# A two-layer graph network kernel: each node number in the count matrix is split at 128 instead of 98

## The reference

```
layer 0:  x_t = mlp(x);  e_t = mlp(edge_attr)
          aggregated = segment_sum(x_t[src] * e_t, dst)
          x = layernorm(x + layernorm(x + aggregated) * gamma + beta)
layer 1:  loops added; deg = segment_sum(1, dst)
          h = x;  twice: h = segment_sum(w[edge] * h[dst], src), w from deg of src and dst
          x = layernorm(x + h @ W.T + b)
```

## Time and profile before

| what | value |
|---|---|
| time, median of 3 runs | 7911.91 us (7910.12 to 7913.29) |
| the profiled execution's own time | 7922.12 us |
| its span in the profile | 7920.4 us |
| PE busy | 6220.9 us (79%) |
| PE weight loads busy | 5013.7 us (63%) |
| DVE busy | 4907.6 us (62%) |
| ACT busy | 4014.2 us (51%) |
| POOL busy | 3681.7 us (46%) |
| SP's DMA queue, share of 16 engines | 91.5% |
| packets under 512 B | 2152641 of 2451761 |

### The profile page before, as it was taken

One profiled execution on the slowest core, in us unless ns is written; L12 is line 12 of the kernel. 1 busy time (PEld: TensorE's weight loads), 2 busy tenths in 40 slices (PEclk: granted clock), 3 DMA queues, 4 the chain that ended last, 5 costly groups with the idle time before them and its releaser, 6 DMA issues.

```text
span 7920.4 us, 153799 instructions
## 1 busy us (share of the span) xinstructions
PE 6220.9 (79%) x51112; PEld 5013.7 (63%) x51113; DVE 4907.6 (62%) x6884; ACT 4014.2 (51%) x6632; POOL 3681.7 (46%) x3315
## 2 busy tenths in 40 slices
PE   6567776777776777777777777777389999999999
PEld 3455555555554555555555555555279999999998
DVE  3566666666666666667776767676745555455554
ACT  1444444444444444444444444444257767666665
POOL 0776666666666666666676666666010000100000
PEclk9665666666666666666666666666599999999999
DMA  3899999999999999999999999999566666666665
GB/s 114 56 72 69 72 70 71 72 68 71 69 71 71 68 71 71 68 72 68 71 68 68 68 69 67 69 67 70 37 183 199 196 188 198 199 185 186 188 190 160
DMA packets 2451761, 809.65 MB, mean 102 GB/s; under 512 B 2152641, under 2 KB 2378105, under 8 KB 2451049
## 3 DMA queue, kind: packets, MB, share of 16 engines
q1 hardware_dynamic: 2317110, 677.47, 91.5%
q0 software_dynamic: 107552, 121.32, 17.1%
q10 hardware_dynamic: 27018, 9.90, 0.5%
HBM read 590.00 MB, written 218.34 MB: 102 GB/s over the span
## 4 chain that ended last, share of the span: by engine, by line
PE 42%; SPq 40%; DVE 6%; ACT 4%; issue 3%; DMA 3%; POOL 1%; ACTq 0%; DVEq 0%; POOLq 0%
SPq L495 40%; PE bank L935 13%; PE compared L935 7%; PE sums L426 4%; PE compared L870 4%; PE bank L857 3%; PE sums L935 3%; PE bank L838 3%; DVE U L1198 2%; ACT arena L671 2%; DMA arena<-counts 1%; POOL arena L574 1%; PE bank L851 1%; ACT U L653 1%; ACT arena L739 1%
## 5 line engine op out<-in xcount | busy, mean ns | idle before, releaser
L574 POOL DMA_INDIRECT arena<-node_rows,arena x3125 | 3480.4, 1114 | 1895.1 <-issue 916.7
L671 ACT ACTIVATE arena<-compared 128x392 uint8<-128x392 f32 x3936 | 1749.6, 498 | 1719.9 <-PE compared L870 1327.9
L870 PE MATMUL compared<-U 128*128 128x98 bf16 x15744 | 1572.0, 256 | 1229.9 <-ACT arena L671 878.2
L870 PEld LDWEIGHTS compared<-U 128*128 128x128 bf16 x15744 | 1087.1, 120 | 1733.5 <-ACT arena L671 1193.8
L739 ACT ACTIVATE arena<-arena 128x1792 bf16<-128x1792 uint8 x868 | 1470.1, 1696 | 706.4 <-DMA arena<-counts 370.0
L1287 DVE CAST arena<-arena 128x1792 bf16<-128x1792 uint8 x868 | 947.5, 1094 | 998.1 <-PE sums L935 629.2
L935 PE MATMUL bank<-arena 128*128 x13888 | 1448.9, 248 | 0.0
L1198 DVE TENSOR_TENSOR U<-iota_share,arena 128x2048 bf16<-128x2048 bf16 x984 | 1197.4, 1217 | 93.1 <-PE compared L870 93.1
L935 PEld LDWEIGHTS bank<-arena 128*128 128x128 bf16 x13888 | 1187.6, 99 | 2.4
L935 PE MATMUL compared<-arena 128*128 x6944 | 1151.4, 248 | 42.6 <-DMA arena<-hop_parts,first_dst 25.0
L1198 DVE TENSOR_TENSOR U<-iota_b,arena 128x1568 bf16<-128x1568 bf16 x984 | 950.0, 965 | 0.0
(11 more groups left out here) (193 smaller groups left out, 3925.8 us busy)
## 6 DMA issues: line engine op xcount, KB each, us to landing
arena<-counts SPq DMA_DIRECT2D x1736, 224.0 KB
counts<-arena SPq DMA_DIRECT2D x124, 1568.0 KB, 6.5
arena<-in_edge_attr SPq DMA_DIRECT2D x125, 448.0 KB
arena<-node_rows,arena POOLq DMA_INDIRECT x3125, 17.4
hop_parts<-arena ACTq DMA_DIRECT2D x14, 672.0 KB, 5.2
arena<-in_x_t SPq DMA_DIRECT2D x13, 256.0 KB, 2.7
node_rows<-H SPq DMA_DIRECT2D x1, 3136.0 KB, 16.5
edge_rows<-arena SPq DMA_DIRECT2D x1, 3125.0 KB
```

What stands on the lines that cost most here:

```text
L574: e.indirect_dma_start(out=rows[:, q, k, :], out_offset=None, in_=node_rows, in_offset=bass.IndirectOffsetOnAxis(ap=src_i[:, t:t + 1], axi ...
L671: nc.scalar.activation(stage[:, k, v:v + VB, :].rearrange("p v n -> p (v n)"), compared[:, c % 2, 0:VB * B], ACT.Copy).then_inc(s_ev, 1)
L870: mm = nc.tensor.matmul(compared[:, c % 2, n * B:(n + 1) * B], HOH[:, j % 2, VB * c + n, :], BOH[:, j % 2, VB * c + n, :], start=True, sto ...
```

## The change

Before, high = n div 98 (0 to 127) and low = n mod 98 (0 to 97). Now high = n div 128 (0 to 97) and low = n mod 128. The stationary matrix of a row's product, the one-hot of the high digit, has 98 columns instead of 128, and the moving one has 128 instead of 98. The product has 98 partitions of 128 numbers instead of 128 partitions of 98. A fill is 98 x 512 instead of 128 x 392, and a block's store consists of 98 x 128 pieces of 128 bytes instead of 128 x 128 pieces of 98 bytes. The digits are now made with a shift and a mask. `stage` grows into the space of `raw`, which is not in use then, and the zero tile for the last, empty block is half as long and lies elsewhere.

```diff
-        STAGE_W = 2 * P * B // 4
-        stage = place_in_arena(STAGE_W).bitcast(u8).rearrange("p (q v n) -> p q v n", q=2, n=B)
+        STAGE_W = 2 * P * P // 4
+        stage = place_in_arena(STAGE_W).bitcast(u8).rearrange("p (q v n) -> p q v n", q=2, n=P)
...
-        ZW = COLS // 4
-        zero_t = arena[:, AT_RAW:AT_RAW + ZW // 4].bitcast(u8)
+        ZW = COLS // 8
+        zero_t = arena[:, AT_EA + EA_W:AT_EA + EA_W + ZW // 4].bitcast(u8)
...
-        HOH = U_flat[:, 0:V * P].bitcast(bf16).rearrange("p (q v e) -> p q v e", q=2, e=P)
-        BOH = U_flat[:, V * P:V * P + V * B].bitcast(bf16).rearrange("p (q v e) -> p q v e", q=2, e=B)
+        HOH = U_flat[:, 0:V * B].bitcast(bf16).rearrange("p (q v e) -> p q v e", q=2, e=B)
+        LOH = U_flat[:, V * P:2 * V * P].bitcast(bf16).rearrange("p (q v e) -> p q v e", q=2, e=P)
...
             def store_block(k, q):
                 e.wait_ge(s_ev, last_use(k) + (1 + 2))
-                e.dma_start(counts[bass.ds(k * P, P), :].rearrange("v (a b) -> a v b", b=B), stage[:, q, :, :])\
+                e.dma_start(counts[bass.ds(k * P, P), :].rearrange("v (a b) -> a v b", b=P), stage[0:B, q, :, :])\
                     .then_inc(s_cst[q], 16)
...
-                    nc.scalar.activation(stage[:, k, v:v + VB, :].rearrange("p v n -> p (v n)"),
-                                         compared[:, c % 2, 0:VB * B], ACT.Copy).then_inc(s_ev, 1)
+                    nc.scalar.activation(stage[0:B, k, v:v + VB, :].rearrange("p v n -> p (v n)"),
+                                         compared[0:B, c % 2, :], ACT.Copy).then_inc(s_ev, 1)
...
-                        mm = nc.tensor.matmul(compared[:, c % 2, n * B:(n + 1) * B], HOH[:, j % 2, VB * c + n, :],
-                                              BOH[:, j % 2, VB * c + n, :], start=True, stop=True)
+                        mm = nc.tensor.matmul(compared[0:B, c % 2, n * P:(n + 1) * P], HOH[:, j % 2, VB * c + n, :],
+                                              LOH[:, j % 2, VB * c + n, :], start=True, stop=True)
...
-            link(nc.vector.tensor_scalar(whole, src_g[0:G, :], 1.0 / B, -(B - 1) / (2.0 * B), ALU.mult, ALU.add))
...
+            for n, (op, by) in enumerate(((ALU.arith_shift_right, 7), (ALU.bitwise_and, P - 1))):
+                link(nc.vector.tensor_scalar(digit[n][0:G, :], src_g[0:G, :], by, None, op))
+                node_leaky(2 + 2 * n, 3 + 2 * n)
+                link(nc.vector.tensor_scalar(table_part(P + n * (P // 2)).bitcast(bf16), by_tile(digit[n][0:G, :]),
+                                             (1.0 / P, 1.0)[n], None, ALU.mult))
+                node_leaky(3 + 2 * n, 4 + 2 * n)
...
-                for c, (to, iota, w) in enumerate(((HOH, iota_share, P), (BOH, iota_b, B))):
+                for c, (to, iota, w) in enumerate(((HOH, iota_share, B), (LOH, iota_b, P))):
```

More of the change, by code:

```diff
@@ L1080, in _ @@
             e.wait_ge(s_gsrc, 16)
-            whole = quotient[0:G, :].bitcast(i32)
-            link(nc.vector.tensor_scalar(whole, src_g[0:G, :], 1.0 / B, -(B - 1) / (2.0 * B), ALU.mult, ALU.add))
-            node_leaky(2, 3)
-            link(nc.vector.scalar_tensor_tensor(out=remains[0:G, :], in0=whole, scalar=-float(B), in1=src_g[0:G, :],
-                                                op0=ALU.mult, op1=ALU.add))
-            node_leaky(3, 4)
-            link(nc.vector.tensor_scalar(above[0:G, :], remains[0:G, :], float(B), 1.0 / P, ALU.is_ge, ALU.mult))
-            node_leaky(4, 5)
-            link(nc.vector.scalar_tensor_tensor(out=table_part(P).bitcast(bf16), in0=by_tile(whole), scalar=1.0 / P,
-                                                in1=by_tile(above[0:G, :]), op0=ALU.mult, op1=ALU.add))
-            node_leaky(5, 6)
-            link(nc.vector.scalar_tensor_tensor(out=table_part(P + P // 2).bitcast(bf16), in0=by_tile(above[0:G, :]),
-                                                scalar=-float(B * P), in1=by_tile(remains[0:G, :]),
-                                                op0=ALU.mult, op1=ALU.add))
-            node_leaky(6, 7)
+            for n, (op, by) in enumerate(((ALU.arith_shift_right, 7), (ALU.bitwise_and, P - 1))):
[4 more added lines that the diff above has]
+                node_leaky(3 + 2 * n, 4 + 2 * n)
             nc.vector.tensor_copy(table_part(0, 1), by_tile(dst_g[0:G, :])).then_inc(s_table, 1)
-            node_leaky(7, 8)
+            node_leaky(6, 8)
             link(digits_of_first(False, low_digit, 0))
```

17 lines of the change are left out of this document (8 added, 9 removed).

## The result

| | before | after |
|---|---|---|
| median, four runs of each on the same chip | 7911.01 us | 7791.95 us |
| ratio, with its 95% interval | | 0.985 (0.9833 to 0.9867) |
| span of the profiled execution | 7920.4 us | 7790.6 us |
| mean granted clock of PE | 0.74 | 0.777 |

The account below looks back on a forecast made before the run. The store's 41 to 43 us was taken to pace the first stage, the engines the second. Loop -62.9 us (342 regained, 283 spent on fills), +9 outside: net -54, from 7911.9 to 7858 us; range 7740 to 7945.

Parts of the forecast that it names:

- The store: SP's queue: a block's store falls from 41.0 us to 31 or less, bounds 16.5 and 41.0, and leaves the chain.
- the estimate of 35.9 us from 14 engines: Store DMA: 31.4 us at today's price a piece becomes 35.9 if 98 partitions run on 14 engines instead of 16.
- the last rival: Loop: fewer DMA waits also bring gathers earlier, or the fills' growth is under 1.8 us a group; 7780 us, chance 0.05.
- The copy: ACT's copy of a fill grows from 498 to 597 ns, +0.10 us, with 512 numbers a partition instead of 392.
- batches 2 and 3: Fill run at PE's lower clock level, ending with the turning of the keys: grows by about 0.9 us.
- the load: PE's weight load before a fill's first matmul: 0.02 us more at each exposed fill, 0.15 a group; bounds nothing and 0.1.
- The base of the first stage: First-stage group without the wait for the store, before larger fills: 38.5 us, range 37.3 to 39.2.
- a rival at 0.16: PE's clock rises more often because PE is busier; 1 us less a group, 7735 us, chance 0.16.
- x: Growth of a group from larger fills, copies and weight loads: 2.3 us; the change breaks even at 2.74.
- the fills win back everything: All 32 copies' 0.10 us lie on the path, growth 3.2 us a group; slower or even, 7969 us, chance 0.17.
- The start: The four groups outside the loop grow by 2.3 us each, +9 us.
- the stated 36.6 to 40.8: POOL, next in line in the loop, needs 36.6 us of a 44.15 us group and stays below 40.8.

Follow-up runs that it names:

- e4: Changed kernel with the whole of counts shifted by 30 bytes in DRAM, so that the 128-byte pieces are unaligned; 7822.4 us.
- e5: Changed kernel without the gathers of tiles 7, 15 and 23 of each group (three of POOL's 25); 7831.5 us.
- e16: Changed kernel with the wait for the free bank put ahead of the wait for DVE's marks in batches 1 and 5, no extra matmuls; 7808.5 us.
- e2: Changed kernel with the stationary one-hot weights padded with zeros from 98 to 128 columns; 7797.3 us.
- e1: Kernel before, storing only half of each block (partitions 64 to 127 left out); 7670.9 us.
- e6: Kernel before with half of each store left out and without the gathers of tiles 7, 15 and 23 of each group; 7592.2 us.
- e3: Changed kernel whose fill matmuls move 98 columns instead of 128, copies still 512 long; 7905.8 us.
- e9: Changed kernel with eight extra 128 x 128 matmuls in PE's wait for DVE's marks in batches 1 and 5, free bank waited for first; 7571.6 us.
- e14: Kernel before with half of each store left out and eight extra matmuls in each of batches 1 and 5; 7563.9 us.
- e7: Changed kernel with 98 moving columns instead of 128 and without the gathers of tiles 7, 15 and 23 of each group; 7900.3 us.
- e15: Changed kernel with 98 moving columns instead of 128 and eight extra matmuls in each of batches 1 and 5; 7839.8 us.
- e10: Changed kernel with weights padded to 128 columns and eight extra matmuls in each of batches 1 and 5; 7525.4 us.
- e17: Changed kernel with weights padded to 128 columns, extra matmuls in batches 1 and 5, and without the gathers of tiles 7, 15 and 23; 7289.2 us.

## Why the prediction was right and wrong

**The store: right that it leaves the chain, wrong on its price.** SP waits for blocks, ACT no longer waits for landings. It took 12.6 us, under the lower bound of 16.5, and the estimate of 35.9 us from 14 engines was far off, since the price was not by piece. The prediction held any value up to 31 to be the same. e4, the changed kernel with a store of 34.4 us, is 30 us slower than after in the first stage and 7 in the start, so a hidden store still costs something; this is what the last rival named (gathers that come earlier, 0.05). It is no fixed price: e5 and e16, with stores as short as after's, needed 41.04 and 41.03 us a group.

**The copy, batches 2 and 3, and the load: right in their sizes or nearly.** 594 ns for 597; 0.93 us for 0.9; the load grew by 37 ns where 20 were put, within the bounds. By full weights e2 gained 1.04 us a group in the second stage, which its clock shares in, and nothing in the whole.

**The base of the first stage: wrong.** The prediction took ACT's wait off in full (43.0 - 4.8), put 38.5 and kept 37.3 to 39.2. Its lowest reading, 37.3, is of groups that follow a wait of 17 us at the start (below), and no steady pace. Without the store's wait the loop takes 39.78 (e1), 39.28 when POOL is relieved (e6). Part of the removed wait came back as others, DVE's 91.7 us for edge rows among them. This alone would have made the kernel slower than predicted, by 1.28 x 76 = 97 us. With the right base the forecast would have been a kernel slower by 43 us, so it was luck that it came as near as it did.

**The clock: the step that failed, as the second stage shows it.** The sum priced the fills at today's clock and left the rise to a rival at 0.16, with the reason that the runs keep their waits. The granted clock rose by 0.06 and 0.04, beyond the 0.03 that the prediction named as its own refutation. The size of it, from pairs with and without the extra matmuls in the second stage: after (45.92 - 42.98) / 0.10, half store (44.20 - 42.16) / 0.07, full weights (44.88 - 42.25) / 0.10, so 0.26 to 0.29 us a group for each 0.01. Against e16, which has the same order of waits, after's pair gives 0.25; the pair with 98 moving columns gives 0.44, over 0.04 of clock only. e3 gives it without extra matmuls: 1.71 us more than after, and 0.6 that its smaller products should have saved, for 0.09 of clock, 0.26. The second stage of after, against e1's, is then +1.72 = x - 4 x 0.29, and **x is near 2.9, not 2.3**, an estimate; with 0.25 it is 2.7, with 0.44 3.5, and e9 against e14 gives 0.82 + 7 x 0.29 = 2.85 (2.6 with 0.25). So x is above 2.3 by each of them, and the refund of the clock at least 1.0 us a group, by 0.29 1.2, where the rival put 1. Whether x passes the 2.74 from which the rival "the fills win back everything" decides is not settled. The gain beyond the forecast in the second stage is the difference of the two errors: +0.6 of fills and -1.16 of clock make -0.56; -0.53 was measured against 46.45, 23 us over the stage. Half of the clock's refund was hidden by a price that was too low, which is luck again.

**The first stage: the size is measured, its parts are not settled.** From e1 to after the fills cost 0.68 us net where 2.3 were put; from e6 to e5, with POOL relieved in both, 1.76. The 1.08 between them is the 0.50 that POOL costs e1 and the 0.58 by which after lies below e5. A clock higher by 0.03 can't be much of it: with the order of waits the same, e16 to e9, 0.13 of clock gave 1.80 us there, 0.14 for each 0.01. Nor is e1's store as short as after's (18.8 us on SP's queue), and its DVE waits 91.7 us for edge rows. Six kernels (e2, e3, e5, e7, e15, e16), among them products of three shapes, took 41.01 to 41.05 us a group there, and after took 40.46. In such a locked pace a price does not show one to one. Here e5's stores, 40.67 and 41.26 apart in turn:

```profile
2032.78 0.36 SPq L499 DMA_DIRECT2D counts<-arena  x1
...
2073.45 0.36 SPq L499 DMA_DIRECT2D counts<-arena  x1
...
2114.71 0.36 SPq L499 DMA_DIRECT2D counts<-arena  x1
```

What sets this pace, and why after leaves it, stays open, and with it the cause of the 31 us of this stage. That the gathers don't set it is shown by e5.

**The start: wrong sign.** It was to share the growth of the fills and fell by 11.4 us. A small transfer of edge rows on the chain of before, and then the keys on DVE that wait for the same one, before and after:

```profile
287.87 17.23 DMA arena<-edge_rows,row_tile
```

```profile
305.22 0.35 DVE L1184 SCALAR_TENSOR_TENSOR key<-arena,row_dst 128x128 bf16<-128x128 f32 x1 [18.48 <-DMA arena<-edge_rows,row_tile]
```

```profile
290.89 0.35 DVE L1174 SCALAR_TENSOR_TENSOR key<-arena,row_dst 128x128 bf16<-128x128 f32 x1 [0.54 <-DMA arena<-edge_rows,row_tile]
```

It took 17.23 us while the first store (issued at 275.81) was under way; after, it was issued at 284.43, 6.5 us into the first store, and DVE's keys could begin at 290.89. In e1, with half that store, it took 12.88, and the store of block 2 came at 364.26, 7.5 us earlier than before; in e4, with the long store, that store came at 367.38, 7 us later than after's. The prediction looked at the store only as something its own queue waits for. The rest of the 11.4 us was not separated.

**POOL: right as far as it went.** In the first stage of after it had no idle time but that of issue and was yet not the bound (e5). With the clock up it is: e10 needs 39.18 us a group and e17 36.36, and 39.2 lies inside the stated 36.6 to 40.8.

## What to carry to other kernels

Where PE falls back to 1.2 GHz in short waits, the price of an edit is not only what it adds but what it does to those waits: look at PEclk stage by stage, and try filling a known wait with matmuls into a bank that PE already owns (here -220 us). When a wait is subtracted, keep a margin for the waits behind it, and look for small transfers that a large one delays, also where the large one itself is hidden. And make a DMA's pieces whole and aligned before counting them: the same bytes took 12.6, 21.9, 34.4 or 40.5 us.

## What the hardware showed unexpectedly

- Whole aligned 128-byte pieces cost 1.0 ns each over all engines, the same pieces shifted by 30 bytes 2.7, and 98-byte pieces 2.5 with no straddling at all. The Trainium skill (DMA: Bandwidth & Descriptors, section "Specifications") says that a transfer below 512 bytes is done as a read-modify-write. No run here shows whether that happens; the times show that pieces below 512 bytes differ by a factor of 2.7 with their length and alignment.
- Less work in each product made the kernel slower (e3, +114 us), through a granted clock of 0.61; more work made it faster (e9).
- A gather on POOL took 0.94 us in most rows and up to 5.2 us beside DVE's marks; that it is DVE's marks which stretch it is read from their overlap and was not tried.

```profile
2023.09 1.99 POOL L573 DMA_INDIRECT arena<-node_rows,arena  x1 [0.30 <-issue]
2025.39 5.19 POOL L573 DMA_INDIRECT arena<-node_rows,arena  x1 [0.30 <-issue]
```
